# Attention layer with one latent key and value per token: two attends in a row on TensorE, in place of one in each of four slots

## What is computed

```python
B, S, d = X.shape
H = NUM_HEADS            # 4
dk = d // H              # 32
scale = 1.0 / jnp.sqrt(jnp.float32(dk))
nx = _rmsnorm(X, g1)
Q = (nx @ Wq.T).reshape(B, S, H, dk).transpose(0, 2, 1, 3)
Kc = nx @ Wkc.T
Vc = nx @ Wvc.T
scores = jnp.einsum('bhsd,btd->bhst', Q, Kc) * scale
attn = jax.nn.softmax(scores, axis=-1)
out = jnp.einsum('bhst,btd->bhsd', attn, Vc)
out = out.transpose(0, 2, 1, 3).reshape(B, S, d) @ Wo.T
X = X + out
```

## Time and profile before

| | |
|---|---|
| median of 3 runs | 2715.28 us (2713.32 to 2717.45) |
| profiled execution, its time | 2702.93 us |
| profiled execution, its span | 2701.1 us |
| TensorE busy | 2417.3 us, 89% of the span |
| VectorE busy | 1928.1 us, 71% |
| ScalarE busy | 1413.1 us, 52% |
| POOL busy | 1453.0 us, 54% |
| first `attn0` loop, scores of step 0 to the last `end` product | 284.19 to 447.29 us |
| second `attn0` loop, the same | 789.22 to 952.32 us |
| scores of step 3 to scores of step 4 | 342.17 to 363.10 us |

### The profile page before, as it was taken

How to read it: one execution, slowest core, us unless ns; L and a number is a source line. 1 busy time by engine, 2 the same in 40 slices (tenths; PEclk the granted TensorE clock), 3 DMA queues, 4 the chain that set the end, 5 groups by cost and what they waited for, 6 DMA issues and landing times. The chain is left out here.

```text
span 2701.1 us, 40094 instructions
## 1 busy us (share of the span) xinstructions
PE 2417.3 (89%) x12716; PEld 1529.1 (57%) x12716; DVE 1928.1 (71%) x4454; ACT 1413.1 (52%) x2280; POOL 1453.0 (54%) x1357
## 2 busy tenths in 40 slices
PE   4477997998789889979999989998999999979999
PEld 3344564666756566644444467776444444447777
DVE  6865775775677667756666578887787778758887
ACT  4642454333435533346666455554677677655554
POOL 5924654333365634356666545554776576425554
PEclk8788898998979989999999999998999999989999
DMA  1001111221011022210000021110000000022221
GB/s 48 0 3 29 36 37 57 95 89 56 1 47 42 14 93 91 95 57 1 1 1 1 26 84 64 56 56 32 1 1 1 2 1 1 1 79 68 71 67 44
DMA packets 57513, 104.50 MB, mean 39 GB/s; under 512 B 15192, under 2 KB 30424, under 8 KB 57048
## 3 DMA queue, kind: packets, MB, share of 16 engines
q1 hardware_dynamic: 57304, 101.90, 12.0%
HBM read 86.53 MB, written 2.62 MB: 33 GB/s over the span
## 5 line engine op out<-in xcount | busy, mean ns | idle before, releaser
L4469 POOL TENSOR_TENSOR l_moe1sc<-l_moe1s,l_moe1bcs 128x512 f32<-128x512 f32 x192 | 281.5, 1481 | 223.3 <-ACT l_moe1s L4291 204.0
L2327 DVE TENSOR_REDUCE l_diffneg_max<-psum 128x1 fp32r<-128x512 f32 x512 | 335.3, 685 | 92.1 <-PE psum L2065 84.2
L2242 ACT ACTIVATE l_diffweights<-psum 128x1024 f32<-128x1024 f32 x256 | 262.0, 1026 | 131.6 <-PE psum L2094 130.4
L4291 ACT ACTIVATE l_moe1s<-psum 128x512 f32<-128x512 f32 x256 | 152.5, 597 | 212.2 <-PE psum L851 209.3
L4380 DVE TENSOR_TENSOR x<-l_moe1sc,psum 128x512 f32<-128x512 f32 x256 | 174.6, 682 | 97.6 <-POOL l_moe1sc L4469 57.1
L2065 PE MATMUL psum<-l_diffkz,l_diffQ 128*128 128x512 f32 (+1 forms) x512 | 234.9, 477 | 3.8 <-DVE l_diffneg_max L2327 2.7
L2866 ACT ACTIVATE l_lightswapped<-psum 32x512 f32<-32x512 f32 x304 | 179.0, 589 | 100.9 <-DVE l_lightturned L2958 97.4
L4387 DVE TENSOR_TENSOR l_moe1g_lo<-x,l_moe1g_hi 128x512 fp32r<-128x512 f32 x256 | 221.7, 867 | 0.4 <-ACT l_moe1g_hi L4266 0.2
L1592 DVE TENSOR_REDUCE l_attn0neg_max<-psum 128x1 fp32r<-128x512 f32 x256 | 167.3, 683 | 52.8 <-PE psum L1326 50.1
L1498 ACT ACTIVATE l_attn0weights<-psum 128x1024 f32<-128x1024 f32 x128 | 130.3, 1024 | 120.4 <-PE psum L1348 120.4
L4291 ACT ACTIVATE l_moe0s<-psum 128x512 f32<-128x512 f32 x144 | 85.8, 596 | 200.0 <-PE psum L851 178.1
(11 more groups left out here) (584 smaller groups left out, 6706.4 us busy)
## 6 DMA issues: line engine op xcount, KB each, us to landing
l_moe0bcs<-gate_rows SPq DMA_DIRECT2D x64, 512.0 KB, 4.5
l_moe1bcs<-gate_rows SPq DMA_DIRECT2D x64, 512.0 KB, 3.9
l_attn0Q<-l_attn0q_hi SPq DMA_DIRECT2D x128, 64.0 KB, 2.0
l_moe1w_raw<-in_moe_w SPq DMA_DIRECT2D x20, 256.0 KB, 6.9
l_attn0Q<-l_attn0q_lo SPq DMA_DIRECT2D x64, 64.0 KB, 2.0
l_moe0w_raw<-in_moe_w SPq DMA_DIRECT2D x20, 128.0 KB, 5.1
x<-in_x SPq DMA_DIRECT2D x8, 256.0 KB, 5.0
out<-x SPq DMA_DIRECT2D x8, 256.0 KB, 2.3
```

The source lines that it names most:

```text
L2242: nc.scalar.activation(weights[:, tt, 2 * pair:2 * pair + 2, :], ps[:, S[m % 2]:S[m % 2] + 2, :], ACT.Exp, scale=SCALE).then_inc(act_exp.s ...
L2327: nc.vector.tensor_reduce(neg_max[:, n % 2, st, row:row + 1], ps[:, bank_of(("max", n, b)), :], AXX, ALU.max, negate=True).then_inc(vec_ma ...
L4291: nc.scalar.activation(s[:, n % 2, h, :], ps[:, H1[(n * HT + h) % 2], :], ACT.Silu).then_inc(act_silu.sem, act_silu.step("silu", h))
L4469: nc.gpsimd.tensor_tensor(sc[:, n % 2, h, :], s[:, n % 2, h, :], weights_row(n), ALU.mult).then_inc(pool_sc.sem, pool_sc.step("sc", h))
```

## The change

Only the order of TensorE's list in the loop of `attn0_block` changes. The attend tt = 2 of the sequence before moves from slot 0 to slot 2, directly ahead of tt = 3; the attend tt = 0 of the sequence itself moves from slot 4 to slot 6, directly ahead of tt = 1. The first maximum product of the slot stays ahead of the pair, the second behind it. The waits of an attend move with it; for tt = 0 these include the wait for `V` and for ScalarE's copy out of bank 0.

```diff
                 part_max(s, m, 0)
-                if m == 0 and real(s - 1):
-                    attend(s - 1, 2)
                 if m == 1 and EARLY <= s + 2 < NSEQ:
                     values(s + 2)
                 if m == 2 and real(s - 1):
+                    attend(s - 1, 2)
                     attend(s - 1, 3)
                     sums(s - 1)
-                if m in (4, 6) and real(s):
-                    attend(s, (m - 4) // 2)
+                if m == 6 and real(s):
+                    attend(s, 0)
+                    attend(s, 1)
```

## The result

The median went from 2716.36 us (6 runs, 2706.06 to 2726.68) to 2750.10 us (6 runs, 2746.80 to 2750.67). The ratio is 1.0122, with an interval of 1.0096 to 1.0148. The forecast was 2729.7 with a range up to 2738: the direction was right, the size was not, and the time lies outside the range. Against the median of before that the forecast started from (2715.28) it said +14.4, and +34.8 came.

The account below looks back on a forecast made before the run. TensorE sets the pace of the `attn0_block` loop, waiting on ring banks. Terms of +6.6, -0.65 and +1.3 make +7.2 a layer, +14.4 for both; added to the median 2715.28 this gives 2729.7, range 2721 to 2738.

Parts of the forecast that it names:

- The ring: Three PSUM banks: products wait for the bank's last reader; moved attends no longer cover this, +1.38 a steady step.
- the price of a join: TensorE: single attend 1.20, attend with narrow work behind it 0.88, so each join saves 0.32; two joins a step.
- the 1.98 weighed against it: Pair of attends by the skill page's rule, full 0.99 each; the join would save 0.21, steps be 22.5.
- one term left open: Sums of step 6 after POOL wait: if the clock stays up, each layer regains 1.3, total 2727.1; lower clock kept.
- 2 x 0.88 added, 0.23 + 0.15 taken back: Steady step on TensorE: two joined attends add, slots 1 and 5 win little back; +1.38 a step.
- Rival C: With some 3.5 us of waits a step, ring waits grow on themselves; further 0.5 a step, 2738; chance 0.05.
- Step 0: First step of a layer's loop, VectorE starting behind: query product earlier, join adds 0.88; +0.41.
- Step 4: Step with `opening.statistics` on VectorE; slot 4's attend covers nothing there and gives nothing back: +0.65 + 0.88 = +1.53.
- Step 5: Step whose gate begins POOL's chain for step 6; +0.50 up to its gate product.
- step 7's joins: Step 7, led by scores and exponentials: two joins, each moving what follows by +0.65.
- the rows product of step 6: With slot 4's attend behind it, two exponentials run back to back and the rows' copy follows sooner: -0.65.
- Both layers alike: Both layers run the same code and times, each ending +7.2 late, together +14.4.

Follow-up runs that it names:

- e3: Changed kernel with slot 0's second maximum product computed five times in steps 1 and up, four redundant; 2739.28 against 2721.13 before, ratio 1.0077.
- e1: Kernel before with only the join of slot 6: attend 0 moved from slot 4, attend 2 left in slot 0; 2728.81 against 2721.13, ratio 1.0034.
- e2: Changed kernel with the slot 6 join undone, leaving only the join of slot 2; 2746.37 against 2721.13 before, ratio 1.0096.
- e4: Changed kernel with VectorE's key subtraction and normalising multiply put ahead of the first maxima of slots 0 and 4; 2724.66 against 2721.13 before, ratio 1.0009.
- e8: e3 with two redundant products in place of four; one run, 2727.90 against a median of 2720.88 before.
- e6: e4 with the tail add of slot 7 also put ahead of the second maximum on VectorE; 2728.67 against 2720.88 before, ratio 1.0025.

## Why the prediction was right in its steps and wrong in its sum

**Right, with sizes.** The ring: +1.38 a steady step was forecast, e3 shows +1.41 with the clock held (22.34), e1 shows one half, +0.66, and e2 the other where the clock held, +0.73 in step 4. Slot 1's first maximum product at 2.84 behind the scores waits for the key subtraction, slot 5's at 2.39 for the normalising multiply. The printed waits (0.81 and 0.74) are a little below the 1.0 and 0.9 that I named, but the starts are right to 0.02. The pair takes 1.74 at full clock, so the price of a join was right and the 1.98 weighed against it did not come.

**The step that failed** is the one named "one term left open". It asked for the granted clock only behind the two long waits of steps 6 and 7 (3.57 and 1.83), and took full clock everywhere else, as in the rows of before. The sum "2 x 0.88 added, 0.23 + 0.15 taken back" prices the joined attend of slot 2 at the full clock. It ran at the lower clock for most of its length (0.57 over 353.51 to 356.52): 3.01 to the sums where 1.75 was due, and the two scores and the maximum product ahead of it were slow already (352.29 to 353.51). Against the forecast that is 1.6 to 1.7 in each of steps 1 to 4, 1.4 on average for each of the seven falls of a loop, 9.9 of the first loop's 16.0. I had the new wait of slot 1 ("about 1.0") in my own working and did not ask what a step with an attend less ahead of its narrow products does to the clock, though the same rows showed the clock dropping behind a wait. Rival C had the right end (2738, "worse than read") with a chance of 0.05, but another mechanism: ring waits that grow. The runs show none; TensorE idles 2.1 in the changed step, not the "some 3.5" of that rival.

**Smaller terms of the first loop.** Step 0: 0.41 forecast, 0.03 measured. Step 4: 1.53 forecast, 3.22 measured, which is 1.53 and one fall. Step 5: 0.50 up to its gate product was forecast; the whole step is 4.41 longer and has two falls, one in slot 2 and one in slot 6 (3.07 at 415.17). Steps 6 and 7 together: the loop's 16.0 less the 16.7 of steps 0 to 5 leaves -0.7. In step 6 I kept the lower clock for the sums; it was the open term's other side that came (TensorE, changed kernel):

```profile
427.05 1.95 PE L1370 MATMUL psum<-l_attn0half_sums,l_attn0pick 128*32 128x128 f32 x64 [1.19 <-POOL l_attn0half_sums L1719]
```

The wait is 1.19 (3.57 in the earlier trace rows, about 2.4 expected) and the sums take 1.95 instead of 3.21, the 1.3 that the open term named. The sums come at 427.05 instead of the forecast 419.8, and the layer ends at 462.25, not near 454.9 (the forecast's own +7.2 on 447.29 gives 454.5); both are late by the falls. The remainder, 0.65 for step 7's joins and -0.65 for the rows product of step 6, lies in that -0.7 with one more fall (3.39 at 441.11) and can't be taken apart from these traces.

**Both layers alike** was nearly right (16.0 and 17.2), but e3, e4 and e8 show that two loops of the same code can differ by a fall or by several.

**What stays open.** Which property of the stretch ahead decides on the fall isn't settled. With the attend of slot 0 in place there was none ahead of the sums in 60 steps. With it gone, a longer hole went with more falls (10 and 6 of 10 at 0.8 to 1.0, 3 of 10 at 0.3 to 0.6), the same hole brought one in one step and not in the next (e2, e8), and 4 of the 20 steps of e4 and e6 had one with hardly a hole. So the hole makes the fall more likely and isn't needed for it; only redundant work in its place left none (e3). The hole of slot 5 went with no fall in steps 1 to 4 of e1. A kernel with the narrow value products taken out of slot 1 and the hole left was not run.

## What to carry to other kernels

A piece of work that waits for nothing is cover for the buffers being read around it: before moving it, list for each product that then follows directly when its buffer's last reader ends, and put that reader ahead on its own engine if it can go there. Price every new wait of TensorE twice, for its length and for the clock of the work behind it, and give the second its own term wherever the trace of before shows the clock dropping behind any wait at all. Closing the wait need not bring the clock back: what fills the place of the moved work counts too. Where a loop's clock is in play, compare loops of the trace, not totals, and repeat a gain of 0.2% before believing it.

## What the runs showed of the hardware

The granted clock fell to 0.50 for at least 3 us (353.00 to 356.00) inside a step in which TensorE was busy 21.82 of 23.93 and no printed wait was longer than 0.81. I had expected a fall only behind waits like the 3.57 of step 6. In e6 it fell with no wait longer than 0.22 ahead of it in the step. Filling 0.94 of that step with redundant products kept it at 1.00 and took 15 of the 33.7 us back. Filling half, which left holes of 0.33, kept it up in some steps and not in others, and there the fall came earlier and lasted longer (clock 0.50 over 328.00 to 334.40 of e8, about 4 behind the step's start, where that of the changed kernel begins 5.5 behind), and cost more (25.55 against 22.32, 3.2).

The Trainium skill (TensorE: Matmul & The Clock Gate, "A second HAM failure mode: psum-queue depth-cycling") describes a kernel that goes round PSUM banks and whose short idles between groups of matmuls make the clock go back and forth. The steps here agree in kind, with holes of 0.2 to 0.8 and a clock of 0.93 over the step. So does e3, where the ring is as late and only the idle time is gone; the falls of e4 and e6 at 0.2 of idle time say that the idles aren't all of it.

The later, untouched layer took 492.2 to 504.6 in traces of kernels that are identical there, at a granted clock of 0.98 and 0.95. That is a scatter of 12 us that does not follow the change: e8, which contains it, has 492.2 like the kernel before.
